# Transposing the shifted scores ahead of the next query projection in two cross-attention stages

## The reference

```python
q = (query @ W_q.T).reshape(B, Sq, H, dh).transpose(0, 2, 1, 3)
k = (key @ W_k.T).reshape(B, Skv, H, dh).transpose(0, 2, 1, 3)
v = (value @ W_v.T).reshape(B, Skv, H, dh).transpose(0, 2, 1, 3)
scores = jnp.einsum('bhqd,bhkd->bhqk', q, k) / jnp.sqrt(jnp.asarray(dh, q.dtype))
attn = jax.nn.softmax(scores, axis=-1)
out = jnp.einsum('bhqk,bhkd->bhqd', attn, v)
...
x = x + _L0_xattn_ref(_layernorm(x, axis=-1), ctx_1024, ctx_1024, ...)
x = x + _L0_ffn_ref(_layernorm(x, axis=-1), ...)
x = x + _L1_xattn_ref(_layernorm(x, axis=-1), ctx_1024, ctx_1024, ...)
x = x + _L1_ffn_ref(_layernorm(x, axis=-1), ...)
```

## Time and profile before

| | |
|---|---|
| median of 3 runs | 556.78 us (554.17 to 560.02) |
| profiled execution, device time | 556.78 us |
| its span, first to last instruction | 555.0 us |
| mean granted TensorE clock | 0.938 of 2.4 GHz |
| PE busy | 490.9 us, 88% |
| DVE, ACT, POOL busy | 295.5, 190.6, 215.0 us |

### The profile page before, as it was taken

How to read it: one execution, slowest core, us unless ns; L and a number is a source line. 1 busy time by engine, 2 the same in 40 slices (tenths; PEclk the granted TensorE clock), 3 DMA queues, 4 the chain that set the end, 5 groups by cost and what they waited for, 6 DMA issues and landing times. The chain is left out here.

```text
span 555.0 us, 9556 instructions
## 1 busy us (share of the span) xinstructions
PE 490.9 (88%) x3126; PEld 395.7 (71%) x3126; DVE 295.5 (53%) x671; ACT 190.6 (34%) x426; POOL 215.0 (39%) x291
## 2 busy tenths in 40 slices
PE   4799998399999997899999999999456999998587
PEld 3577775267787775568999999999334776675475
DVE  4688885552163121325554455554234588986483
ACT  2446453175530020102333323333112464452053
POOL 3210240233333566308985533333223554510074
PEclk9999998769999999899999999999855899999799
DMA  8998100110000222699613332221165000000013
GB/s 304 398 397 210 3 0 1 53 34 1 1 1 30 81 89 102 186 327 350 108 49 97 105 88 77 79 68 39 38 202 178 0 2 1 2 1 1 0 40 114
DMA packets 48352, 53.52 MB, mean 96 GB/s; under 512 B 14737, under 2 KB 42706, under 8 KB 48050
## 3 DMA queue, kind: packets, MB, share of 16 engines
q1 hardware_dynamic: 33794, 22.49, 14.7%
q0 software_dynamic: 7152, 19.67, 10.4%
q10 hardware_dynamic: 7360, 10.75, 6.1%
HBM read 35.78 MB, written 17.12 MB: 95 GB/s over the span
## 5 line engine op out<-in xcount | busy, mean ns | idle before, releaser
L130 POOL TENSOR_TENSOR rstd<-var,mhalf 128x2 f32<-128x2 f32 x32 | 22.5, 704 | 131.8 <-DVE var L123 131.8
L426 DVE TENSOR_REDUCE mx<-banks 128x16 f32<-128x1024 f32 x32 | 39.0, 1220 | 32.5 <-PE banks L287 32.4
L1133 PE MATMUL banks<-w_hi,xgT_hi 128*128 x156 | 54.8, 352 | 1.2 <-ACT xgT_hi L821 1.1
L1299 DVE TENSOR_TENSOR hgT_lo<-banks,hgT_hi 128x256 fp32r<-128x256 f32 x78 | 24.1, 351 | 56.4 <-ACT hgT_hi L987 55.0
L980 ACT ACTIVATE hg<-banks 128x352 f32<-128x352 f32 x39 | 18.1, 464 | 97.7 <-PE banks L1137 87.0
L1134 PE MATMUL banks<-wd,xgT_hi 128*128 x156 | 50.4, 324 | 0.0
L1070 PE MATMUL banks<-sdn,big 128*128 128x256 f32 x192 | 47.6, 394 | 0.0
L1057 PE MATMUL banks<-xn2T_hi,sgu_hi 128*128 128x512 f32 (+1 forms) x96 | 39.7, 414 | 5.7 <-DVE big L1265 5.0
L287 PE MATMUL banks<-kvb,qT 64*128 64x256 f32 x256 | 38.2, 418 | 7.1 <-DVE ps L429 2.9
L141 ACT ACTIVATE xn<-x,shift,rstd 128x256 f32<-128x256 f32 (+1 forms) x64 | 34.9, 600 | 28.0 <-POOL shift L132 25.9
L1070 PEld LDWEIGHTS banks<-sdn,big 128*128 128x128 f32 x192 | 34.0, 189 | 12.8 <-issue 9.3
(11 more groups left out here) (216 smaller groups left out, 1110.1 us busy)
## 6 DMA issues: line engine op xcount, KB each, us to landing
w_hi<-in_egu POOLq DMA_DIRECT2D x2, 2816.0 KB, 20.7
expert_rows_in<-zeros SPq DMA_DIRECT2D x1, 5304.0 KB, 41.7
xn<-expert_rows_in SPq DMA_DIRECT2D x39, 128.0 KB
y_all<-choices_out SPq DMA_DIRECT2D x16, 256.0 KB, 4.9
wd<-in_egu ACTq DMA_DIRECT2D x8, 352.0 KB, 9.4
wd<-in_egu ACTq DMA_DIRECT2D x4, 704.0 KB, 12.2
out_x<-fo SPq DMA_DIRECT2D x8, 256.0 KB, 2.2
x<-in_x ACTq DMA_DIRECT2D x2, 768.0 KB, 10.8
```

What stands on the lines that cost most here:

```text
L426: nc.vector.tensor_reduce(mx, heads(psS), AX.X, ALU.max).then_inc(max_done.sem, 1)
L1133: nc.tensor.matmul(to, xgT_hi[:, c, k, :], hi, start=(k == 0), stop=False)
```

## The change

Two steps trade places, one on PE and one on ACT, in both attentions. On PE `transpose_s(u, 0, 0)` and `transpose_s(u, 0, 1)` come before `project_q(u + 1)`, no longer behind it. On ACT `exps(u, 0, 0)` and `exps(u, 0, 1)` come before `copy_q(u + 1)`. No instruction is added or taken away, and no wait is changed. DVE, POOL and SP keep their orders.

```diff
@@ PE
                 other_work("tensor", 2 * u)
                 scores(u, 1)
-                if u + 1 < NU:
-                    project_q(u + 1)
                 if u == 0:
                     pe.wait_ge(kv.done, kv.all)
                 transpose_s(u, 0, 0)
                 transpose_s(u, 0, 1)
+                if u + 1 < NU:
+                    project_q(u + 1)
                 other_work("tensor", 2 * u + 1)
@@ ACT
                 if u >= 1:
                     inverse(u - 1)
+                exps(u, 0, 0)
+                exps(u, 0, 1)
                 if u + 1 < NU:
                     copy_q(u + 1)
-                exps(u, 0, 0)
-                exps(u, 0, 1)
                 if u + 2 < NU:
                     normalise(u + 2)
```

## The result

| | before | changed |
|---|---|---|
| median | 557.0 us (4 runs, 554.17 to 560.02) | 565.98 us (4 runs, 565.11 to 566.87) |
| ratio of the runs | | 1.0129, 95% interval 1.0080 to 1.0178 |
| span of the profiled execution | 555.0 us | 565.8 us |
| mean granted TensorE clock | 0.938 | 0.939 |

What follows compares the result with a forecast made beforehand. PE's row of instructions was taken to bound the attention passes. Twelve passes at 0.88 (10.6 us), nothing for u = 4 and 0.8 for u = 0 of attn1 gave 11.4 us, so 568.1 us, range 563.5 to 573.5.

Steps and rivals of the forecast that it cites:

- The bound: Attention passes: as long as PE's row of instructions, PE busy all of 9.98 us in attn0; DVE waits for PE.
- The cover: End of a pass: eight transposes hide ACT's 0.60 us copy; moved ahead, they leave PE idle 0.7 to 0.9 us.
- The exponentials: On ACT: earlier start counts nothing; their 1.08 us fits within the projection's 1.99, so the copy is not late.
- The price of the step, 0.88 a pass: Transposes in series on PE, between 0.83 and 0.93: steady passes of 10.86 us in attn0, 10.99 in attn1; 12 pay.
- the 2.80 us from projection to scores: End of a pass: projection to copy 2.03, copy 0.60, hand-over 0.17; claimed to stay as they are.
- Pass u = 4 of attn1: Bound by DVE at 11.36 us, above the 10.99 the copy would allow; claimed to pay nothing.
- Pass u = 0 of attn1, 0.8: Half-clock pass: with the clock rising at about 434.7, scores come at 436.59 against 435.77, a loss of 0.8 us.
- The sum: All 14 passes: 10.6 + 0 + 0.8 = 11.4 us, span from 555.0 to 566.4, time 568.1 us.
- The gaps marked as issue: Rival: PE's idle gaps, such as 0.33 ahead of the transposes, shrink and win the stall back; 556.8 us, chance 4%.
- The clock: Rival: new PE stalls drop it to half in two passes, 5 us each; 578 us, chance 6%.
- The dear transposes, 1.26: Rival: each pass pays the upper price, 0.93 plus an idle gap of 0.33; 573.6 us, chance 8%.
- The spread that I put on half-clock stretches, 2 us either way: Stretches at half clock, like the 3.57 us projection in attn0's tail, can fall otherwise when all shifts: some 2 us.

Runs made afterwards that it cites:

- pe_only: Kernel before with only PE's half: first tile's transposes ahead of the projection, ACT's order as before; 564.22 us, ratio 1.0148.
- half_cover: Changed kernel with four of the eight transposes back behind the projection, and the copy between the two exponentials on ACT; ratio 1.0039 to the kernel before.
- act_only: Kernel before with only ACT's half: exponentials ahead of the copy, PE's order as before; 573.08 us, ratio 1.030.
- doubled: Kernel before with each of the first tile's eight transposes done twice in seven passes of each attention; 567.65 us, ratio 1.0235.
- warm_after: Changed kernel with 30 matmuls of no use in PE's idle time at the end of the experts and start of attn1; ratio 1.0111 to the kernel before.
- warm_before: Kernel before with 30 matmuls of no use in PE's idle time at the end of the experts and start of attn1; ratio 0.9967.
- after_again: The changed kernel run once more against the kernel before; 560.54 against 553.19 us, ratio 1.0141.
- attn0_only: Kernel before with the whole change in attn0 only, attn1 as before; 557.77 us, ratio 1.0052.
- attn1_only: Kernel before with the whole change in attn1 only, attn0 as before; 558.67 us, ratio 1.0060.
- warm_more: Kernel before with 30 matmuls of no use around attn1's start and 35 more in waits at both attentions' ends and before the shared expert; ratio 0.9879.

## Why the prediction was right, and where it was off

**The bound.** Right: PE's row of instructions is the pass. Doubled transposes cost their own time, and DVE moved out of the way as said.

**The cover.** Right: the transposes hid the copy, and without them PE waits for it in 13 of the 14 passes, all but the one that DVE bounds, for 0.69 us in attn0 and 0.93 in attn1 (0.7 to 0.9 were forecast). `pe_only` shows that this is PE's order alone, `half_cover` that the loss follows what is left of the cover.

**The exponentials.** Right that their earlier start is worth nothing and their new place no burden. `act_only` shows that the second holds only as long as the transposes go first too.

**The price of the step, 0.88 a pass.** Mis-sized. It is 0.82 us in attn1, the step by the weight loads: the projection's first load starts 0.82 behind the transposes, and I had taken the middle to the 0.93 of the matmuls. The Trainium skill's rule that PE pulls weight loads ahead of matmuls ("TensorE: Matmul & The Clock Gate", section "Architectural detail: the array is 16× 32×32, not 1× 128×128"), by which the prediction had 0.83, gave the better value, and in attn1 the trace agrees with it. In attn0 it is 0.71. There the 2.80 us from projection to scores, which I held fixed, shrank: they contained 0.17 us between the end of the copy and the scores, and that hand-over takes 0.05 in the changed profile. So what the prediction had wrong is which of two waits ended last: it took the copy, but in the old order attn0's scores came 0.12 later than the copy allowed, held by PE's own eight transposes ahead of them. `doubled` lengthens just this step, by 0.87 in attn0 and, where the longer copy left 0.13 of slack, by 0.74 in attn1. The profile names the copy as the releaser, as it came last of the semaphores; that PE's own row was what ended last, by 0.12, it doesn't say. A steady pass of attn0 is therefore 10.70 us and not within the 10.8 to 10.9 of the forecast; attn1's 10.94 is near the 10.99.

**Pass u = 4 of attn1** pays nothing. Right, down to L1366.

**Pass u = 0 of attn1, 0.8.** The transposes do cost their time here too, but the 0.8 came from a clock that I had fixed in time, and that part did not hold. At half clock on both sides it was 12.64 - 11.47 = 1.2 us: by the granted clock it rose 11.1 us behind the pass's first scores (0.50 up to 439.0, 0.89 from there to 439.5) and not 10.7 (0.52 in 434.5 to 435.0). At the full clock on both sides (`warm_after` and `warm_before`) it is 8.62 - 7.79 = 0.83. Over all profiles the pass took between 7.8 and 12.6 us, which is more than the term.

**The sum.** By the passes it is 7 x 0.71 + 5 x 0.82 + 0.8 = 9.9 us in place of 11.4. Between the two profiles the attentions grew by 4.97 us (from the first scores to the last second scores of attn0: 71.95 to 76.92) and by 5.25 (attn1: 78.70 to 83.95), 10.2 in all, and the spans by 10.8. So the forecast of 11.4 has two errors on the same side, 1.5 us in the passes and some 2 outside of them, and that the four runs of the result came within 2.1 us of the 568.1 is in part luck.

**The rest.** The runs put the loss at 7 to 8 us: ratios 1.0129 and 1.0141 here, 1.0144 and 1.0131 with fillers, each with 9.9 us (1.018) at the edge of its interval or just outside, and all four on the same side. Some 2 us seem to come back outside the steady passes. The experiments side by side (us; attn1's first pass counted at one clock throughout; mean clock of the runs):

```
                by passes   by the ratio          clock before, this
after_again        9.9       7.8 (5.3 to 10.3)      0.946   0.952
pe_only            9.9       8.2 (3.7 to 12.7)      0.944   0.946
act_only          17.7      16.7 (13.3 to 20.0)     0.944   0.947
attn0_only         5.0       2.9 (0.8 to 5.0)       0.944   0.950
attn1_only         4.9       3.3 (1.0 to 5.7)       0.944   0.949
half_cover         4.2       2.2 (0.4 to 3.9)       0.946   0.950
doubled           10.6      13.0 (10.1 to 15.9)     0.946   0.945
```

In all six that fall short, the runs had a mean clock 0.001 to 0.006 above that of the kernel before beside them. In `doubled`, the one with a lower clock, the ratio lies above the passes. If the clock is what differs, it is worth 1.1 to 1.8 us of the shortfall in `after_again`, `attn0_only`, `attn1_only` and `half_cover`, at 3.0 to 3.4 us for each 0.01. Only a small part of the higher clock follows from the longer passes themselves: by an estimate 10 us more at the full clock raise the mean by 0.001.

One source shows in the profiles: the output projection at attn0's end, ran at half clock in the four profiles with the old order in attn0 and no fillers there (3.26 to 3.65 us), and at the full clock in the eight in which attn0 was longer, for whatever reason. A kernel of each kind, both from the timeline:

```profile
93.98 3.65 PE L319 MATMUL banks<-wo,big 128*128 128x256 f32 x8 [0.95 <-DVE big L441]
...
103.04 1.78 PEld L319 LDWEIGHTS banks<-wo,big 128*128 128x128 f32 x8 [4.03 <-DVE big L441]
```

```profile
98.23 2.00 PE L319 MATMUL banks<-wo,big 128*128 128x256 f32 x8 [0.96 <-DVE big L447]
...
105.64 2.39 PEld L319 LDWEIGHTS banks<-wo,big 128*128 128x128 f32 x8 [4.04 <-DVE big L447]
```

From attn0's last second scores to the shared expert's first transposes it is 21.8 to 22.6 us in the four and 20.2 to 21.6 in the eight, 1.2 less on the average. So where no fillers stand there, this would give back a good half of the missing 2 us, by one profile of each kernel. But with fillers this stretch is 20.40 and 20.39 in both orders, and the loss stayed at 7.2 us, though with an error of 2. So this is not shown to be the whole cause. What else gives time back stays open: the experts' stage between the attentions varies by several us from one profile to the next of the same program, and hides it.

**The rivals.** The gaps marked as issue did not give the stall back (0.33 stands behind the wait as before, at 56.88). The clock stayed at 1.00 in all passes of the changed kernel that began at it, in both of its profiles. It did fall in attn0's first pass in the profiles of `act_only`, `half_cover` and `warm_more`; the last has the old order, so the new one is not needed for it. The rule of the Trainium skill ("TensorE: Matmul & The Clock Gate", section "Why this matters for your kernels") that short gaps leave the clock up agrees with the steady passes, with their waits of 0.69 and 0.93 us, but not with attn0's end in the old order, where TensorE came to half clock behind waits of 1.56 and 0.95 us. The dear transposes, 1.26, did not come. The spread that I put on half-clock stretches, 2 us either way, was about right: 318.1 and 314.3 us between the attentions in two profiles of the kernel before.

## What to carry to other kernels

Work that stands between a producer and the consumer of its copied result may be all that hides the copy: before moving it, compare its time with the copy's, and if PE is busy for the whole pass, expect to pay the moved work in full, less the time by which it outlasted the copy (here 0.82 us a pass for 0.82 us of transposes in attn1, and 0.71 in attn0). A wait that the profile names, and that lasts 0.1 or 0.2 us, says which semaphore came last, not that the engine's own row had slack. And where a kernel's runs spread by 1%, the lengths of single passes show a change of 0.1 us that the total can't.

## What was not expected of the hardware

- Steady passes of one order repeat to 0.02 us over all profiles, while the total of the kernel before varies by 5 to 8 us on one chip, and much of that goes with the mean granted clock: 2.5 to 3.4 us for each 0.01 on the four chips of the experiments (correlations of -0.68 to -0.89), 3.4 over the 21 executions of the changed kernel (-0.93).
- Ahead of attn1 PE stands idle for some 11 us (10.90) and then runs its matmuls at half clock, 1.2 GHz: the eight for the keys (L166) take 2.04 us, against 1.13 behind fillers. How long it stays there differed between executions of the same program: attn1's first pass took 12.64 and 8.61 us in two profiles of the changed kernel.
- 65 matmuls of no use in PE's idle time raised the mean clock from 0.947 to 0.987 (means of the runs) and made the kernel 1.2% faster (interval 0.9 to 1.5%), with nothing else changed.
